# First layer's mean squares by one multiply with a row sum, not by batch statistics

## The reference

```
layer 0:  h = film(rmsnorm(x, w1), cond);  x = x + attention(h)        one head
          h = film(rmsnorm(x, w2), cond);  x = x + mlp(h)              128 -> 512 -> 128, gelu
layer 1:  h = modulate(layernorm(x), cond);  x = x + gate * attention(h)   16 heads, masked
          h = modulate(layernorm(x), cond);  x = x + gate * mlp(h)
rmsnorm(x, w) = x * rsqrt(mean(x * x, over channels) + 1e-6) * w
```

## Time and profile before

| what | value |
|---|---|
| median of 3 runs | 177.9 us (177.57 to 178.03) |
| the profiled execution | 177.6 us |
| its span | 175.8 us, 5695 instructions |
| busy: PE, PEld | 169.6 us (96%), 132.5 us (75%) |
| busy: DVE, ACT, POOL | 113.4 us (64%), 109.2 us (62%), 106.9 us (61%) |
| granted clock of TensorE | 1.0 in the whole span |

### The profile page before, as it was taken

One profiled execution on the slowest core, in us unless ns is written; L12 is line 12 of the kernel. 1 busy time (PEld: TensorE's weight loads), 2 busy tenths in 40 slices (PEclk: granted clock), 3 DMA queues, 4 the chain that ended last, 5 costly groups with the idle time before them and its releaser, 6 DMA issues.

```text
span 175.8 us, 5695 instructions
## 1 busy us (share of the span) xinstructions
PE 169.6 (96%) x2244; PEld 132.5 (75%) x2244; DVE 113.4 (64%) x350; ACT 109.2 (62%) x282; POOL 106.9 (61%) x175
## 2 busy tenths in 40 slices
PE   6999999999999999999999999999999999999994
PEld 6986876794585988886688877888788765769594
DVE  0577899584014567798766876688888647695333
ACT  2588888907856262675676757668767796532600
POOL 5587989899935409719323434669989776690000
PEclk9999999999999999999999999999999999999999
DMA  4999999916963001100110010100000000001103
GB/s 106 370 413 438 412 414 421 395 39 130 188 229 142 4 2 65 62 6 6 65 63 5 6 45 20 65 6 6 4 7 6 6 2 4 0 0 60 63 0 119
DMA packets 5478, 19.31 MB, mean 110 GB/s; under 512 B 588, under 2 KB 1564, under 8 KB 4124
## 3 DMA queue, kind: packets, MB, share of 16 engines
q1 hardware_dynamic: 5132, 18.66, 29.2%
q10 hardware_dynamic: 320, 0.29, 0.6%
HBM read 7.24 MB, written 1.09 MB: 47 GB/s over the span
## 4 chain that ended last, share of the span: by engine, by line
PE 91%; DVE 3%; ACT 2%; issue 1%; DMA 1%; POOL 0%; POOLq 0%; DVEq 0%
PE ps L417 21%; PE ps L483 9%; PE ps L337 8%; PE ps L365 8%; PE ps L345 8%; PE ps L374 7%; PE ps L253 4%; PE ps L259 3%; PE ps L494 3%; PE ps L397 2%; PE ps L400 2%; PE ps L505 2%; PE ps L404 2%; PE ps L318 2%; PE ps L298 1%; DVE nm L1118 1%
## 5 line engine op out<-in xcount | busy, mean ns | idle before, releaser
L1118 DVE TENSOR_REDUCE nm<-ps 128x4 f32<-128x512 f32 x64 | 42.0, 683 | 16.8 <-PE ps L417 16.4
L835 ACT ACTIVATE shared<-ps 128x512 f32<-128x512 f32 x64 | 35.4, 601 | 16.3 <-PE ps L417 16.3
L417 PEld LDWEIGHTS ps<-k_pad,q_pad 32*128 32x128 f32 x512 | 29.7, 186 | 9.2 <-issue 5.8
L417 PE MATMUL ps<-k_pad,q_pad 32*128 32x128 f32 x512 | 35.0, 282 | 1.0 <-DVE nm L1118 0.5
L417 PE MATMUL ps<-q_pad,k_pad 32*128 32x128 f32 x512 | 35.1, 283 | 0.1
L417 PEld LDWEIGHTS ps<-q_pad,k_pad 32*128 32x128 f32 x512 | 29.4, 186 | 0.5 <-DMA q_pad<-nmT 0.3
L1244 POOL TENSOR_TENSOR rstd<-var_eps,half 128x4 f32<-128x4 f32 x16 | 16.4, 1023 | 19.7 <-DVE var_eps L965 16.5
L1329 POOL TENSOR_TENSOR gated<-attn,gate 128x128 f32<-128x128 f32 x16 | 7.4, 460 | 21.6 <-ACT attn L854 21.4
L483 PE MATMUL ps<-shared,vx 128*32 128x128 f32 x512 | 17.3, 275 | 0.1
L885 ACT ACTIVATE hid<-ps,W 128x512 f32<-128x512 f32 x16 | 10.9, 689 | 9.7 <-PE ps L365 9.7
L365 PE MATMUL ps<-hT,W 128*128 128x512 f32 x32 | 15.3, 599 | 0.0
(11 more groups left out here) (156 smaller groups left out, 335.5 us busy)
## 6 DMA issues: line engine op xcount, KB each, us to landing
q_pad<-gate SPq DMA_DIRECT2D x1, 4096.0 KB, 21.5
k_pad<-gate SPq DMA_DIRECT2D x1, 4096.0 KB, 30.7
gate<-gates SPq DMA_DIRECT2D x1, 2048.0 KB, 14.5
xs<-x SPq DMA_DIRECT2D x4, 256.0 KB, 5.8
gate<-mask SPq DMA_DIRECT2D x1, 1024.0 KB, 11.8
q_pad<-apT SPq DMA_DIRECT2D x4, 256.0 KB, 2.4
k_pad<-apT SPq DMA_DIRECT2D x4, 256.0 KB, 2.6
W<-weights SPq DMA_DIRECT2D x1, 768.0 KB, 9.9
```

The lines of the kernel that those rows point to most:

```text
L417: return mm(bank(to)[:, t], held[some, t, b], moved[some, t, b], start=True, stop=True, skip_group_check=True)
L835: a(pT[b % 2][:, r], bank(of), ACT.Exp, scale=HD ** -0.5).then_inc(s["c_exp"], 1)
L1118: v.tensor_reduce(nm[b % 2][:, 4 * r:4 * r + 4], bank(of), AX.X, ALU.max, negate=True).then_inc(s["c_max"], 1)
```

## The change

Each statistic of norms 0 and 1 on VectorE becomes one `scalar_tensor_tensor` that multiplies a batch of `xs` by itself, scaled by 1/128, and writes the row sum into `var_eps`; the products themselves go to a scratch tile, `gmul[0][:, 0]`, the same for all, so each waits for the one before. In the loop all four now stand ahead of `a_turn(g)`. `bn_aggr`, L959 and L961 go for k < 2. Epsilon is added on POOL, in `root`, by a small `tensor_scalar` for every group of norms 0 and 1 (before, only for groups 0 and 1 of norm 0). ScalarE's squares take the scale 128^-1/2 and write their sums into `var_eps` directly. Norms 2 and 3 keep the batch statistics.

```
+            def mean_square(dst, src, signal):
+                v.scalar_tensor_tensor(out=gmul[0][:, 0], in0=src, scalar=1.0 / C, in1=src, op0=ALU.mult, op1=ALU.mult,
+                                       accum_out=dst).then_inc(signal, 1)
+
+            def mean_squares(k, g):
+                base = stats_base(k, g)
+                for j in range(G):
+                    if base + j:
+                        dve.wait_ge(s["stats_ok"], base + j)
+                    b = G * g + j
+                    mean_square(var_eps[:, k, b:b + 1], xs[:, b], s["stats_ok"])
...
             dve.wait_ge(s["x_in0"], 16)
             for j in range(2):
-                v.bn_stats(bn[:, j], xs[:, j]).then_inc(s["a_first"], 1)
...
+                if j:
+                    dve.wait_ge(s["a_first"], j)
+                mean_square(var_eps[:, 0, j:j + 1], xs[:, j], s["a_first"])
...
-            statistics(0, 2)
+            mean_squares(0, 2)
...
-            statistics(0, 3)
+            mean_squares(0, 3)
             a_turn(0)
             for g in range(1, 4):
                 a_max(g)
                 a_residual(g - 1)
                 dve.wait_ge(s["a_res"], G * g)
-                batch_statistics(1, g - 1, range(G))
+                mean_squares(1, g - 1)
                 a_turn(g)
-                moments(1, g - 1)
             a_residual(3)
             dve.wait_ge(s["a_res"], 4 * G)
-            statistics(1, 3)
+            mean_squares(1, 3)
...
             def root(k, g, signal):
...
+                if k < 2:
+                    if k == 0 and g == 0:
+                        pool.wait_ge(s["a_sq0"], 2)
+                        pool.wait_ge(s["a_first"], 2)
+                    elif k == 0 and g == 1:
+                        pool.wait_ge(s["a_sq"], G)
+                    else:
+                        pool.wait_ge(s["stats_ok"], stats_end(k, g))
+                    ve = var_eps[:, k, G * g:G * g + G]
+                    p.tensor_scalar(ve, ve, 1.0, EPS, ALU.mult, ALU.add).then_inc(s["a_ms"], 1)
+                    pool.wait_ge(s["a_ms"], G * k + g + 1)
```

More of the change, by code:

```diff
@@ L63, in build @@
         var_eps = sb("var_eps", [N, 4, B])
-        mean_sq = sb("mean_sq", [N, G])
         bn = sb("bn", [N, G, 6])
         bn_c = sb("bn_c", [N, 2, 6])
-        square_sum = sb("square_sum", [N, G])
-        first_sum = sb("first_sum", [N, 2])
         stat = sb("stat", [N, B, 2])
@@ L155, in build @@
         names = """x_in0 x_in1 x_in2 x_in3 w_film w_film2 w_attn0 w_ada w_mlp0 w_block1 rows_in mask_in mask_rin gate_out gate_in y_out
-            ident_ok half_ok spare_ok stats_ok fold_mm fold_ok qcol_ok a_xa a_true a_first a_TA a_sq0 a_ms0 a_sq a_ms a_xd a_hd film_mm film_one film_ok silu_e silu_one silu_ok
+            ident_ok half_ok spare_ok stats_ok fold_mm fold_ok qcol_ok a_xa a_true a_first a_TA a_sq0 a_sq a_ms a_xd a_hd film_mm film_one film_ok silu_e silu_one silu_ok
             ada_mm ada_ok gate_ok  wvp_mm wvp_ok bias_ok bcol_ok pbias_ok zero_ok pad_zero aug_ok aug_out aug_in maskb_ok c_vinit c_vzero
@@ L167, in build, with stats_base @@
         PER_GROUP = 2 * G + 2
+        def stats_base(k, g):
+            return G * (G * k + g - 2) if k < 2 else 6 * G + PER_GROUP * g
         def stats_end(k, g):
-            n = G * k + g
-            return PER_GROUP * (n - 1)
+            return stats_base(k, g) + (G if k < 2 else PER_GROUP)
         FILM_BANK = (2, 7)
@@ L726, in _ @@
             for j in range(2, G):
-                a(gtmp[:, j], xs[:, j], ACT.Square, accum_out=first_sum[:, j - 2:j - 1]).then_inc(s["a_sq0"], 1)
+                a(gtmp[:, j], xs[:, j], ACT.Square, scale=C ** -0.5, accum_out=var_eps[:, 0, j:j + 1]).then_inc(s["a_sq0"], 1)
             act.wait_ge(s["w_film"], 16)
@@ L760, in _ @@
             for j in range(G):
-                a(gtmp[:, j], xs[:, G + j], ACT.Square, accum_out=square_sum[:, j:j + 1]).then_inc(s["a_sq"], 1)
+                a(gtmp[:, j], xs[:, G + j], ACT.Square, scale=C ** -0.5, accum_out=var_eps[:, 0, G + j:G + j + 1]).then_inc(s["a_sq"], 1)
             act.wait_ge(s["fold_mm"], 1)
@@ L937, in batch_statistics @@
             def batch_statistics(k, g, js):
-                base = stats_end(k, g) - PER_GROUP
+                base = stats_base(k, g)
                 if base:
@@ L956, in moments @@
                 dve.wait_ge(ok, base + 2 * G)
[L957 to L965, removed]
+                v.tensor_copy(mean[:, 0, G * g:G * g + G], agg[:, :, 0]).then_inc(ok, 1)
+                v.tensor_scalar(ve, agg[:, :, 1], EPS, None, ALU.add).then_inc(ok, 1)
             def d_norm(g):
```

## The result

The changed kernel takes 181.11 us (median of 5, 180.95 to 181.12), the kernel before 177.9 us (177.43 to 178.04): a ratio of 1.018, 95% interval 1.0161 to 1.0199. It is 3.2 us slower. The forecast was 183.1 us with a range of 179.0 to 186.2, and "slower" with 0.88: the sign and the mechanism came out, the size did not; 2 of the 5.2 us are missing.

A forecast was written before the change was run, and what follows sets the result against it. TensorE, 91% of the chain, was taken to bound the kernel, its L318 waiting for `a_turn`. Multiplies held by POOL make L318 3.25, 3.9, then 5.2 us late; 177.6 becomes 182.8, 183.1 for the median; 8-in-10 range 179 to 186.2.

The forecast's parts named there:

- the mechanism: VectorE beside POOL: an instruction fetching two SBUF operands waits for the end of a POOL instruction that has begun.
- the 5.2 us: First layer, group 2: the last L318 that counts starts at 38.31 for 33.12, 5.2 us late.
- One multiply by itself: VectorE: 0.291 us, plus 0.10 for the sum's read-out, plus 0.04 wait: 0.43 us per step (0.33 to 0.52).
- A blocked multiply: VectorE beside POOL: ends 0.24 us behind the POOL instruction, and POOL's next one starts 0.12 later.
- the turn between two POOL instructions: VectorE beside POOL: a waiting instruction with two SBUF operands gets one turn between two POOL instructions.
- The sum: First layer, stage by stage: L318 3.25 us late in group 0, 3.9 in group 1, 5.2 in group 2.
- start near 20.0: POOL's three `bias_add` beside layer 1, group 0: start near 20.0 us, 18.49 before, and hold up three multiplies.
- No waiting: Rival, chance 0.08: multiplies don't wait for POOL; nothing won or lost at a 0.43 us step, 177.6 to 178.0 us.
- Waiting, but mostly beside the path: Rival, chance 0.10: multiplies wait for POOL, but L318 is only 2 to 3.9 us late, 179.9 to 181.8 us.
- the likeliest case: First layer: waiting for POOL as worked out, chance 0.82, 183.1 us with its own range 180.8 to 186.
- its three reasons: For waiting mostly beside the path: POOL yields when VectorE asks, only 128x512 additions block, or the additions fall elsewhere.
- the clock: Rival: TensorE's clock falls in the new pauses, doubling 2.8 us of work, 186 us; counted in the likeliest case's upper side.

The follow-up runs named there:

- the run with `bcol1` early: Changed kernel with POOL's additions one by one behind a norm each, mask's conversion in the second layer, `bcol1` and two small conversions behind `bias_add(1)`: 179.25 us, ratio 1.0089.

## Why the prediction was right in sign and too large

**The mechanism.** A multiply with two SBUF operands waits for POOL: right, and shown by exchanging one operand. The single row of L959 carried it. The Trainium skill's page "SBUF — State Buffer" (section "Who interferes with whom") calls such contention an exclusive lock, in which whoever issues first holds on and the other blocks. The rows agree, in both directions: POOL's two `xn` beside the multiplies of norm 0 take 0.90 us where they took 0.72, though an addition is held up by 0.03 us only (below).

Two limits remain. L974, which I took for the same case, reads one tensor and two scalars for each row: it is held too, so two tensors in SBUF are not the only form that waits, and no run takes this up. And each multiply and each L959 that was held reads one tensor twice. In no trace did an instruction with two different SBUF tensors meet more than the last 0.06 us of a POOL instruction, the power apart; that these are held as well is not shown.

**One multiply by itself.** I took 0.43 us per step (0.33 to 0.52). It is 0.33 (15.07 to 15.40), the lower bound: the row sum's read-out takes 0.08 but runs inside the multiply's end (15.28 to 15.36, the multiply 15.07 to 15.36), so that nothing is added but the 0.04 between dependent instructions. ScalarE's read-out, from which I took 0.10, was the wrong neighbour. The "Vector Engine (DVE) Microarchitecture Reference" of the Trainium skill ("Points that are easy to get wrong") would have halved the pace; 0.285 and 0.292, the least and the median with two SBUF operands, against 0.286 with one from PSUM show nothing of it.

**A blocked multiply.** I let it end 0.24 us behind the POOL instruction; it ends 0.15 behind, and the next begins 0.04 after that. POOL's additions came 0.03 us further apart (3.82 for three, 3.72 before), not 0.12. And a wait shorter than 0.14 costs nothing, since it hides in the multiply's own lead; I added one to each of POOL's short instructions. Nor is the turn between two POOL instructions sure, as I had it: in group 2 the multiply began 0.05 us before the end of an addition and waited out the conversion behind it as well (32.76 to 34.83); with 0.07 left, in the run with `bcol1` early, it got its turn (20.57 to 20.87).

**The sum.** The step of it that failed is the place of POOL's additions in group 0: "start near 20.0". They started at 18.91, 19.23 in the terms of the execution before, 0.8 early, because the multiplies of group 3's norm 0 ended at 16.03 (16.35) and not at 17.1: 0.3 of it is three shorter steps, 0.1 the shorter end of the blocked multiply, 0.4 POOL's delay ahead of `bias_add(0)`, of which I had assumed 0.5 (to 14.3) and which was 0.1 (13.60 and 0.32, for 13.81). With that the first multiply of group 0 met only the last 0.17 us of an addition, and two whole turns were lost, not three: L317 came 2.1 us late where I had 3.25. In group 1 I had 0.65 more, and it was 1.0; TensorE was then the late one, at the lower clock. In group 2 I had two waits and 1.3 us, addition and conversion; the multiply began with 0.05 us of the addition left, met the conversion at once, and lost 0.6. Together 1.15 - 0.37 + 0.72 = 1.5 us too much at the last L317; of the other 0.5, 0.2 is that the execution started 0.3 early and then lost 0.17 at a transfer of k, and 0.3 that the medians lie closer together (3.2) than the two profiled executions (3.5).

**The rivals.** "No waiting" fell. "Waiting, but mostly beside the path", 179.9 to 181.8 with a chance of 0.10, holds the measured time, as the likeliest case's 180.8 to 186 does. Of its three reasons, that POOL yields and that only the additions block were not what happened: the additions, the conversion of the mask and `bcol1` all blocked a multiply that met them. The third, that they fall elsewhere, is: fewer met one. The waits lie on the path even so. I put too little on that third reason, having computed one arrangement of two engines to a tenth and not asked how the sum moves if the additions come 0.5 us earlier. Of the clock I wrote that "nothing in the rows speaks for it": it did fall, and cost nothing that can be told.

**After 40 us** every row is later by one constant, as forecast, save 0.2 us at the first transfer of k.

## What to carry to other kernels

Before two instructions are replaced by one, count the SBUF operands of the new one: where GpSimd works beside it, a multiply of an SBUF tensor by itself pays up to the length of the longest GpSimd instruction (2.07 us here beside one of 1.91), and then it matters more what stands behind it in its queue than how long it is itself. With one operand from PSUM it was free. When a loss hangs on which instructions of two queues happen to meet, work the sum out for two or three offsets of one queue, and let the range and the likeliest value come from these.

## What was not expected of the hardware

The granted clock fell to 1.2 GHz after a pause of TensorE inside a busy stage (2.02 us ahead of the weight load) in one execution, and in the run with the mask's conversion later too (2.03 us); it did not after 1.59 us in the run with norm 1 alone, nor, by their mean of 1.00, in the other four executions of the changed kernel. Why it falls in some of them and not in others stays open. The row sum adds nothing to a multiply that can be told: 0.33 us from one start to the next, 0.29 for the multiply and 0.04 for the wait. A four-element instruction on VectorE took 1.62 us beside a GpSimd conversion of 1.90: the wait has nothing to do with the size of the one that waits.
